# A DLRM tower on one core: one table fewer by one-hot products, a second held item between two runs of small matmuls, and the dense part in rounded halves

## What is computed

```python
combined = jnp.concatenate([sparse_x, dense_x[:, None, :]], axis=1)     # (2048, 27, 128)
interact = jnp.einsum('bfd,bgd->bfg', combined, combined)
z = interact[:, TRIU_I, TRIU_J]                                          # 351 pairs
h = jnp.concatenate([z, r_dense_x], axis=1)                              # 479
h = jnp.maximum(h @ W_top1 + b_top1, 0.0)                                # 512
h = jnp.maximum(h @ W_top2 + b_top2, 0.0)                                # 256
y = h @ W_top3
```

## Time and profile before

| | us |
|---|---|
| three timed executions | 407.98, 411.75, 408.25 |
| their median | 408.25 |
| the profiled execution | 403.16 |
| its span | 401.4 |
| TensorE matmul busy | 360.7 (90%) |
| VectorE, ScalarE busy | 223.7, 169.4 |
| GpSimd busy | 259.0 (65%) |

### The profile page before, as it was taken

One profiled execution on the slowest core, in us unless ns is written; L12 is line 12 of the kernel. 1 busy time (PEld: TensorE's weight loads), 2 busy tenths in 40 slices (PEclk: granted clock), 3 DMA queues, 4 the chain that ended last, 5 costly groups with the idle time before them and its releaser, 6 DMA issues.

```text
span 401.4 us, 14335 instructions
## 1 busy us (share of the span) xinstructions
PE 360.7 (90%) x6418; PEld 330.1 (82%) x6418; DVE 223.7 (56%) x247; ACT 169.4 (42%) x473; POOL 259.0 (65%) x278
## 2 busy tenths in 40 slices
PE   3887979898989789997999989996999999998987
PEld 2676869797979689896989889895989989897766
DVE  4786699754466524574458735673356744651122
ACT  2444226254526235362544444361444535364522
POOL 6677777777777777777777777777774777710000
PEclk9998999999999969999999999997899999999999
DMA  6777543322233223222323222312221323200000
GB/s 175 233 220 221 161 114 89 87 80 58 65 82 70 60 54 93 59 80 54 80 68 82 79 57 65 85 51 77 54 76 54 80 56 93 58 16 3 3 2 2
DMA packets 17935, 32.03 MB, mean 80 GB/s; under 512 B 5737, under 2 KB 8689, under 8 KB 17873
## 3 DMA queue, kind: packets, MB, share of 16 engines
q0 software_dynamic: 8640, 17.71, 17.5%
q1 hardware_dynamic: 8352, 12.60, 10.5%
q10 hardware_dynamic: 880, 0.80, 0.6%
HBM read 31.08 MB, written 0.01 MB: 77 GB/s over the span
## 4 chain that ended last, share of the span: by engine, by line
PE 75%; DVE 8%; DMA 8%; issue 7%; ACT 1%; SPq 0%; DVEq 0%; ACTq 0%
PE x_ps L611 31%; PE tail_ps L684 16%; PE gram_ps L630 12%; PE x_ps L592 8%; DMA hot_in<-in_tbl 8%; DVE onehot L872 7%; PE tail_ps L661 2%; PE tail_ps L653 2%; PE tail_ps L690 2%; DVE hot_lo L858 1%; PE x_ps L721 1%; PE tail_ps L732 0%; DVE zt_lo L466 0%; PE x_ps L715 0%; PE x_ps L716 0%
## 5 line engine op out<-in xcount | busy, mean ns | idle before, releaser
L575 POOL DMA_INDIRECT raw<-in_tbl,ids_sb x270 | 258.1, 956 | 92.7 <-issue 78.9
L872 DVE TENSOR_TENSOR onehot<-ids_wide,row_ps 128x1024 fp32r<-128x1024 int16 (+1 forms) x163 | 183.9, 1161 | 88.3 <-PE x_ps L611 85.4
L611 PE MATMUL x_ps<-onehot,hot_hi 128*128 128x256 f32 x566 | 148.3, 297 | 7.1 <-issue 4.0
L611 PE MATMUL x_ps<-onehot,hot_lo 128*128 128x256 f32 x566 | 141.6, 284 | 0.0
L611 PEld LDWEIGHTS x_ps<-onehot,hot_hi 128*128 128x128 f32 x566 | 108.2, 191 | 11.9 <-issue 5.6
L611 PEld LDWEIGHTS x_ps<-onehot,hot_lo 128*128 128x128 f32 x566 | 108.5, 192 | 1.6 <-issue 1.6
L630 PE MATMUL gram_ps<-xt 128*27 128x26 f32 x4096 | 53.0, 193 | 21.5 <-issue 18.2
L388 ACT COPY xt<-x_ps 128x128 f32<-128x128 f32 (+1 forms) x100 | 45.6, 514 | 61.8 <-PE x_ps L611 61.0
L630 PEld LDWEIGHTS gram_ps<-xt 128*27 128x27 f32 x4096 | 44.1, 105 | 30.5 <-issue 24.5
L410 ACT COPY gram<-gram_ps 128x416 f32<-128x416 f32 (+1 forms) x32 | 16.2, 506 | 68.3 <-PE gram_ps L630 68.3
L819 ACT COPY xt<-x_ps 128x384 f32<-128x384 f32 (+1 forms) x78 | 44.5, 631 | 1.3 <-PE x_ps L592 1.3
(11 more groups left out here) (76 smaller groups left out, 315.6 us busy)
## 6 DMA issues: line engine op xcount, KB each, us to landing
ids_wide<-in_hot_ids SPq DMA_DIRECT2D x18, 256.0 KB
raw<-in_tbl,ids_sb POOLq DMA_INDIRECT x270, 3.0
hot_in<-in_tbl SPq DMA_DIRECT2D x14, 256.0 KB, 3.5
hot_in<-in_tbl SPq DMA_DIRECT2D x6, 320.0 KB, 3.9
weights_in_place<-in_w SPq DMA_DIRECT2D x10, 128.0 KB, 2.8
dense_sb<-in_dense_t ACTq DMA_DIRECT2D x6, 128.0 KB, 2.4
dense_sb<-in_dense_t SPq DMA_DIRECT2D x2, 128.0 KB, 3.6
w1d_sb<-in_w SPq DMA_DIRECT2D x2, 128.0 KB
```

The lines of the kernel that those rows point to most:

```text
L575: nc.gpsimd.indirect_dma_start(out=raw[k][:, f, :], out_offset=None, in_=sources[f], in_offset=bass.IndirectOffsetOnAxis(ap=ids_sb[:, t, f ...
L611: last = nc.tensor.matmul(ps, table[:, chunk_at[j] + c, :], moving[:, c - a, :], start=(c == 0 and table is tables_of[0]), stop=(c == chun ...
L872: nc.vector.tensor_tensor(columns(p), ids_wide[:, it // IDS % IDS_RING, it % IDS, 0:width].unsqueeze(1).to_broadcast([P, n, width]), row_n ...
```

## The change

`HOT` is 9 and `SHARES` is zero for every block: nine tables go by one-hot product in every block, the tenth is gathered in all of them, also in block 0 (272 gathers, 17 for every tile). Between the two gram fills of a first tile a second hot item is computed, and both items are held. The transposes of `("zt", 0)` and `("zt", 1)` are issued alternately, in one step. The dense row is rounded and split like the others (`dense_hi` by ScalarE, `dense_lo` by VectorE), its weights are the fourth part of `w1z`, and its one float32 product becomes three float32r products. `xt` has 27 slots for each sample in place of 32.

```diff
-HOT = 10
+HOT = 9
-SHARES = (0, 1, 1, 1, 1, 1, 1, 1)
+SHARES = (0,) * 8
...
-    layer["h1"].insert(0, ("w", "x", 0))
+    layer["h1"][:0] = [("hi", "x hi", n_kz), ("lo", "x hi", n_kz), ("hi", "x lo", n_kz)]
...
-            held = item_end[pieces[hot[0][0][1]][0]] - hot[0][0][1]
-            slots += hot[:held] + gram_slots(t)
-            slots[-1].append(("held", pieces[hot[0][0][1]][0]))
+            p, it = hot[0][0][1], pieces[hot[0][0][1]][0]
+            held = item_end[it + 1] - p
+            fills_of = gram_slots(t)
+            slots += hot[:item_end[it] - p] + fills_of[:1] + hot[item_end[it] - p:held] + fills_of[1:]
+            slots[-1] += [("held", it), ("held", it + 1)]
...
-        xt = sb("xt", [P, XT * P, SLOTS])
+        xt = sb("xt", [P, XT * P, feats])
+        dense_hi = [sb(f"dense_hi{k}", [P, BLOCK], F32R) for k in range(DENSE)]
+        dense_lo = [sb(f"dense_lo{k}", [P, BLOCK], F32R) for k in range(DENSE)]
...
         def tail_split(dve, h, key):
-            if kind == "zt":
+            if key == ("cols", 0):
+                dve.wait_ge(dense_rounded, h + 1)
+                nc.vector.tensor_tensor(dense_lo[h % DENSE][:, :], dense_sb[h % DENSE][:, :],
+                                        dense_hi[h % DENSE][:, :].bitcast(F32), ALU.subtract).then_inc(dense_split, 1)
+            elif kind == "zt":
...
             def tail_step(h, key, part):
+                if key == ("zt", 1):
+                    return
...
+                    blocks_of = [z_blocks[0][0], z_blocks[1][0]] if j == 0 else [z_blocks[j][part]]
                     for s in range(QUAD):
-                        last = nc.tensor.transpose(
-                            ps[0:of.stop - of.start, s * groups_block:(s + 1) * groups_block],
-                            z[rows, s, of], ident[rows, rows])
+                        for bank_of, (odd, of) in zip((ps, tail_ps[tail_bank["zt", 1]]), blocks_of):
+                            rows = slice(odd * groups_block, (odd + 1) * groups_block)
+                            last = nc.tensor.transpose(
+                                bank_of[0:of.stop - of.start, s * groups_block:(s + 1) * groups_block],
+                                z[rows, s, of], ident[rows, rows])
...
             def last_start(m):
-                nc.tensor.matmul(last_h1[m], w1d_sb[:, of[m]], dense_sb[h % DENSE][:, :], start=False, stop=False)
+                for weights, part in ((w1z_hi, dense_hi), (w1z_lo, dense_hi), (w1z_hi, dense_lo)):
+                    if m == 0:
+                        pe.wait_ge(dense_rounded if part is dense_hi else dense_split, h + 1)
+                    nc.tensor.matmul(last_h1[m], weights[:, n_kz, of[m]], part[h % DENSE][:, :], start=False, stop=False)
...
                     to_xt(copy, first, tiles_block, nf + nh, dense_sb[h % DENSE]).then_inc(dense_copied, 1)
+                    copy(dense_hi[h % DENSE][:, :], dense_sb[h % DENSE][:, :]).then_inc(dense_rounded, 1)
```

More of the change, by code:

```diff
@@ L114, in build @@
              + [("hi", "lo", k) for k in range(n)] for kind, n in (("h1", n_kz), ("h2", m1))}
-    layer["h1"].insert(0, ("w", "x", 0))
-    cuts = {"h1": [0] + list(range(1, len(layer["h1"]) + 1, 3)), "h2": list(range(0, len(layer["h2"]) + 1, 3))}
+    layer["h1"][:0] = [("hi", "x hi", n_kz), ("lo", "x hi", n_kz), ("hi", "x lo", n_kz)]
+    cuts = {kind: list(range(0, len(products_of) + 1, 3)) for kind, products_of in layer.items()}
     parts = {(kind, j): len(z_blocks[j]) if kind == "zt" else len(cuts[kind]) - 1 if kind in layer else 1
@@ L277, in build @@
         with nc.sbuf_tensor("hot_in", [P, chunk_at[nh], P], F32) as hot_in:
-            with nc.sbuf_tensor("weights_in_place", [P, n_kz * d1 + m1 * d2], F32) as weights_at:
+            with nc.sbuf_tensor("weights_in_place", [P, (n_kz + 1) * d1 + m1 * d2], F32) as weights_at:
                 pass
         hot_lo = sb("hot_lo", [P, chunk_at[nh], P], F32R)
-        weights_lo = sb("weights_lo", [P, n_kz * d1 + m1 * d2], F32R)
-        weights_hi = sb("weights_hi", [P, n_kz * d1 + m1 * d2], F32R)
+        weights_lo = sb("weights_lo", [P, (n_kz + 1) * d1 + m1 * d2], F32R)
+        weights_hi = sb("weights_hi", [P, (n_kz + 1) * d1 + m1 * d2], F32R)
         ids_wide = sb("ids_wide", [P, IDS_RING, IDS, BLOCK], I16)
@@ L302, in build @@
         b2_sb = sb("b2_sb", [P, m2])
-        weight_parts = [[t[0:n, k, :] for t in (w1z_hi, w1z_lo, w1z_at)] for k, n in enumerate(kz)]
+        weight_parts = [[t[0:n, k, :] for t in (w1z_hi, w1z_lo, w1z_at)] for k, n in enumerate(kz + [P])]
         weight_parts += [[t[:, k:k + 2, :] for t in (w2_hi, w2_lo, w2_at)] for k in range(0, m1, 2)]
@@ L314, in gathers_by @@
             return sum(gathered[:h * tiles_block]) + share * sum(gathered[h * tiles_block:(h + 1) * tiles_block])
-        n_loads = 2 * n_kz + m1 + 2
+        n_parts_h1 = n_kz + 1
+        n_loads = 2 * n_parts_h1 + m1 + 2
         shared_from = (tiles - 1) * n_gram
-        n_others = 5
-        second = [("gram", gram_block + n) for n in range(len(weight_parts) - n_kz)]
-        round_at = [("hot", item_start[nh + 2 + n]) for n in range(n_kz)] + second
-        split_at = [("gram", n_gram + n // 2) for n in range(n_kz)] + second
+        n_others = 3
+        second = [("gram", gram_block + n) for n in range(len(weight_parts) - n_parts_h1)]
+        round_at = [("hot", item_start[nh + 2 + n]) for n in range(n_parts_h1)] + second
+        split_at = [("gram", n_gram + n // 2) for n in range(n_parts_h1)] + second
         x_ps = [psum(f"x_ps{b}", [P, BANK]) for b in range(3)]
@@ L355, in build @@
         dense_copied = sem("dense_copied")
+        dense_rounded = sem("dense_rounded")
+        dense_split = sem("dense_split")
         gram_cleared = sem("gram_cleared")
@@ L655, in tail_step @@
                 elif kind == "zt":
-                    odd, of = z_blocks[j][part]
                     if part > 0:
                         pe.wait_ge(rest_turned, h + 1)
-                    rows = slice(odd * groups_block, (odd + 1) * groups_block)
+                    if j == 0:
+                        other = tail_bank["zt", 1]
+                        reach(pe, tail_copied[other], h * tail_per[other] + tail_nth["zt", 1])
+                    blocks_of = [z_blocks[0][0], z_blocks[1][0]] if j == 0 else [z_blocks[j][part]]
                     for s in range(QUAD):
-                        last = nc.tensor.transpose(
-                            ps[0:of.stop - of.start, s * groups_block:(s + 1) * groups_block],
-                            z[rows, s, of], ident[rows, rows])
+                        for bank_of, (odd, of) in zip((ps, tail_ps[tail_bank["zt", 1]]), blocks_of):
[3 more added lines that the diff above has]
+                                z[rows, s, of], ident[rows, rows])
+                            if s == QUAD - 1 and j == 0 and odd == 0:
+                                last.then_inc(tail_full[kind], 1)
                     if part < parts[key] - 1:
@@ L670, in tail_step @@
                         a, b, k = products_of[n]
-                        if j == 0 and a == "hi":
+                        if j == 0 and b[0] == "x":
+                            pe.wait_ge(dense_rounded if b == "x hi" else dense_split, h + 1)
+                        elif j == 0 and a == "hi":
                             if kind == "h1":
```

25 lines of the change are left out of this document (11 added, 14 removed).

## The result

The changed kernel takes 391.23 us (median of four executions, 390.03 to 395.0), the kernel before in the same comparison 408.12 (404.68 to 411.75): ratio 0.967, 95% interval 0.961 to 0.9725, faster. The profiled executions are 403.16 us before and 390.03 after, with spans of 401.4 and 388.2.

What follows compares the result with a forecast made beforehand. TensorE bounds the kernel, pausing where 256-instruction stretches arrive late; GpSimd is second. Terms sum to −18.7 us, taking the earlier median of 408.25 to 389.5, rounded to 389; range 380 to 400.

Steps and rivals of the forecast that it cites:

- Pauses, −14.3: TensorE's waits for instructions in gram fills: 19.0 us, mostly removed by slow work between a first tile's fills, −14.3 us.
- the prediction's rule: A fill with slow work right before it pauses only where a stretch ends in its last 7 of 256 instructions.
- Clock, −4.4: TensorE's clock no longer falls in blocks 2 and 5 once double pauses go: 2.2 us each, −4.4 us.
- Held copies, +5.4: Blocks 1 to 6: `turn(5,1)` waits 0.9 us for ScalarE to copy the gram and first held item, +5.4 us.
- The share for `h1`, +0.6: ScalarE reaches the `("h1", 1)` copy later, whose bank `("h1", 3)` needs: +0.1 us a block, +0.6 us.
- Tenth table, −3.8: Block 0 loses the tenth table's 20 records and last table load; VectorE's sequence moves up: −3.8 us.
- Dense, −2.6: Dense product of `h1`: one float32 product at 0.44 us becomes three float32r at 0.36 us, −2.6 us.
- Alternating, −0.2: Alternating `zt` transposes may overlap, but `("zt", 2)` still waits for VectorE's split: only −0.2 us, from the last block.
- Gram 28, +0.6: Block 7: three turns of tile 14 right ahead of gram 28 wait for ScalarE's copies, +0.6 us.
- slots of 27, 0: `xt` read and written at steps of 108 bytes instead of 128: 0 us, bounds −1 and +4.
- Gathers: GpSimd: two more gathers, 2.5 us; its 4.34 us wait goes, and the last gather begins near 350 us.
- Rival 3: Gathers come late: at tiles 3 and 4 TensorE is held back 3 to 4 us more, giving 393 us; 8%.

Runs made afterwards that it cites:

- the last fills apart: Changed kernel with second turn later, fill 29 behind the first `h1` parts, last block's first products between fills 30 and 31: 388.37 us, ratio 0.958.
- the shift by 64 instructions: Kernel before, with 32 identity transposes put at the start where TensorE waits anyway: median 401.01 us, against 406.53 before.

## Why the prediction was right, and where its terms were off

The forecast was 389, the median is 391.23, and the range of 380 to 400 holds it. By medians the change is worth 16.9 us where the sum said 18.7. By the two profiled executions it is worth 13.1: that of before was 5.1 us under its median, as the text said, but that of after only 1.2 under its own, so the medians are the better scale.

That the total came so close is in good part luck. The prediction gave the second held item −12.7 us in all (−14.3 for the pauses, −4.4 for the clock, +5.4 and +0.6 for the copies) and everything else −6.0. The runs turn this round: without the item the changed kernel takes 392.73 us, so the rest of the change is worth 15.4 us and the item 1.5, less than the noise. In the kernel before, the item alone brought 0.7%, about 3 us. Two things made most of the difference. The other edits moved the places where instructions arrive, and with that alone the pauses went from 20.1 us (18.2 ahead of gram, 1.93 ahead of `zt`) to 13.9; and the copies cost 9.2 us and not 6.0.

- **Pauses, −14.3: the size and the mechanism right, the credit wrong.** Of the 19.0 us that it counted, 5.1 are left after the change, so −13.9. But the run with one held item has 13.9 us of pauses ahead of gram where the changed kernel has 5.7: the slow work between the fills bought 8.2, and some 6 went with the new places where the stretches end. Fill 20, counted as half a pause, had none; its neighbour 19 had one of 0.94 with eight records, 16 instructions, left, more than the last 7 that the prediction's rule allowed. Those in tiles 14 and 15 stayed, as 1.63 and 2.54 us. The sum passed over one pause: at 57.62 us, in block 0, TensorE stood for 1.50 us ahead of a hot product, at the same place of 256.
- **Clock, −4.4: right in direction, its reason wrong.** That the clock fell "where two pauses came on one another's heels" was misread: in the trace of before it is already down when the second pause begins, at 140.64 us (and in block 5 at 276.45, where the second pause begins at 278.85). In the runs it fell behind single pauses, and also behind waits for other engines alone: at 373.41 us with the last fills apart, in block 1 of three kernels, and in block 0 of most. Single pauses as long, such as the 1.98 us at 186.9 in the kernel before, had no fall behind them. A stretch of 3.41 us at 1.2 GHz costs at most 1.7 us. In the profiled pair the low time went from 17.1 to 3.4 us, which by half of it is up to −6.8, more than was counted; 1.7 of it are the fall in block 0, which the prediction left out, and the one at 351.7 us takes 1.7 from it. The reading of the first fall, in windows of 1 us, the granted clock third from the end:

```profile
139.00:140.00 1.00, 0.95 (x106) 0.86 (x94) 0.42 (x1) 0.25 (x1) 0.84 (x1) 0.96 0.19 41
140.00:141.00 1.00, 0.64 (x34) 0.40 (x24) 0.00 (x0) 0.00 (x0) 0.86 (x1) 0.50 0.24 61
```

- **Held copies, +5.4: the place, the count and the queue right, the size too small.** The price of one wait was right: in blocks 2 to 4 the next transpose starts 0.97 to 0.98 us behind the last where 0.11 is usual, 0.87 lost for the 0.9 of the prediction (0.70 as printed, since a printed wait starts at the end of the last record and not where the next would have started). What it missed is that the waits of blocks 1, 5 and 6 are longer, 1.2 to 1.5 us by the same measure, which makes 6.6 for the six, and that TensorE waits elsewhere too: once more in block 1 (0.50 printed, 0.67 by starts), and some 0.35 us in a block where the turns now start anew. TensorE's time in turns rose by 9.7 in all, and by 9.2 against the run with one held item; +9 would have given 393. The share for `h1`, +0.6, didn't show: it takes 5.96 us in an undisturbed block.
- **Tenth table, −3.8: right as far as the traces tell.** Fill 2 begins 5.1 us earlier than before, up to 1.7 of it by the clock. Undone, it begins 4.6 us later, again up to 1.7 by the clock; the times say 4.2, inside their noise.
- **Dense, −2.6: right, slightly large.** Undone it costs 0.27 us in a block by the trace (the working had 0.32), 2.2 in eight; the medians say 2.2 too, inside their noise. The cast and the subtraction stayed covered.
- **Alternating, −0.2: right.** From the first `zt` transpose to the fill nothing is gained, for the reason given. The −2.9 in the table above went mostly to the hot products ahead of the next transposes: between fills 10 and 14, where no clock fell, the two together take 21.19 us before and 21.05 after.
- **Gram 28, +0.6: 0.29**, and **slots of 27, 0: right** (the earlier trace rows had no such row, the run gives 192 ns for a record at both steps). The estimate of 4 us from the 16-byte lines of the Trainium skill (page "SBUF — State Buffer") is not borne out: fills lost nothing at 27. On the other rule, that crossing a block of instructions is "mostly hidden" (the Trainium skill, page "Runtime: NRT & Kernel Launch", section "Instruction fetch mechanics"), the runs say where it is true: with a stretch of 0.12 us matmuls before them, 128 of which take some 15 us against the 3.7 us of one arrival, the crossings show no pause; with gram in most of the 256 instructions most of them cost 0.4 to 2.6 us. Not all: from 255.74 to 257.98 us the kernel before ran through 256 instructions in 2.24 us without one; why stays open.
- **Gathers: right.** GpSimd's wait of 4.34 us is gone. No wait of TensorE is put down to a gather; only for the 0.50 us before 99.21 us did a gather land as late (99.12) as the copy (99.15). The last gather begins at 353.56 us, 3.6 later than forecast. Rival 3 didn't come here.

The 5.5 us that the shift by 64 instructions won by the medians say something that the prediction didn't see: part of the pauses of before was bad luck in where the stretches ended, and any edit that adds or takes a few instructions deals them anew. So of the 16.9 us some 4 are the tenth table, 2 the dense part, about 6 the new places where stretches end (an estimate from the 20.1 and 13.9 us of pauses), and the second held item is worth 0 to 3. The parts don't add up exactly, since undoing one also moves the stretches for the others; a run of the changed kernel with its old alignment, which would separate them, wasn't made.

## What to carry to other kernels

Where an engine pauses with nothing that it waits for, count its instructions: if the pauses lie at a fixed place of every 256, it runs through short instructions faster than they arrive. The cure is slow work in the same stretch or another alignment; here 64 idle instructions, at a moment when the engine waited anyway, took 5.5 us off the median, while the reordering in the changed kernel took 1.5. Before crediting an edit with fewer pauses, undo it alone: the others may have moved the stretches. Before moving work between two steps, ask what it was covering: work placed against the pauses laid bare waits for copies that cost as much as the pauses had. And where a new wait is for a copy, look at what its engine does first: putting the copies that nobody waits for behind the one that TensorE needs here, together with a later turn, took the ratio from 0.967 to 0.9455 (measured at different times), more than the second held item itself had brought.

## What the runs showed of the hardware

- A pause for instructions is 0.4 to 2.6 us, and begins at instruction 193 or 194 of each 256 in every one of the thirteen traces that have one; the fourteenth, with the last fills apart, has none. Where a stretch ended in a pause, it took 2.9 to 4.2 us from one such place to the next in the kernel before, pause included.
- The same program does not pause at all the same places each time: fill 19 had 0.94 us in one execution and none in the other.
- The clock falls for 3.41 us, or twice that, and needs no long pause: in one run it fell after four waits of 0.34 to 0.93 us within 5 us, 0.85 and then 0.50 in the windows above, in another after a single wait of 1.54 us. Behind the pause of 2.54 us at 367.47 the changed kernel's trace shows no fall. The changed kernel's own four executions have mean clocks of 0.996, 0.991, 0.991 and 0.983, and times that follow them: 390.03, 390.94, 391.52 and 395.0 us.
- Eight transposes of 64 rows in alternating halves of the array are issued in the time of four in one half (0.46 and 0.44 us).
- float32 reads at steps of 108 and of 128 bytes cost TensorE the same; writes at 108 cost ScalarE 0.686 us instead of 0.625 for 128x256.
